# The opening of a cross-attention and FP4 feed-forward kernel: low parts of the down weights by a subtraction on VectorE, and a new order of the opening

## What is computed

```python
def xattn(q, k, v, Wt, Wp, Wg, Wz, gamma, beta):      # k = v = ctx
    t, p, g = Wt @ v, Wp @ q, Wg @ k                  # 256x256 weights over the channels
    att = sum(p * g over each of 8 groups) * 0.125    # one number per group
    y = Wz @ (att * t)                                # per group
    y = (y - mean) / sqrt(var + eps)                  # over a group's channels and columns
    return y * gamma + beta + v
def ffn(x, w_gate, w_up, w_down):                     # 512 -> 1408 -> 512
    q = fp4_quant_dequant                             # blocks of 16, scale max|x|/6, grid 0..6
    h = silu(q(x) @ q(w_gate).T) * (q(x) @ q(w_up).T)
    return q(h) @ q(w_down).T
x = x + xattn(layernorm(x), ctx, ctx, ...)
x = x + ffn(layernorm(x), ...)
```

## Time and profile before

| | us |
|---|---|
| median of 3 runs | 1725.51 (1724.89 to 1725.58) |
| profiled execution, its own time | 1728.17 |
| span of the profile | 1726.1 |
| TensorE busy in the span | 1681.8 |
| VectorE busy | 1503.2 |
| ScalarE busy | 828.3 |
| GpSimd busy | 671.4 |

### The profile page before, as it was taken

How to read it: one execution, slowest core, us unless ns; L and a number is a source line. 1 busy time by engine, 2 the same in 40 slices (tenths; PEclk the granted TensorE clock), 3 DMA queues, 4 the chain that set the end, 5 groups by cost and what they waited for, 6 DMA issues and landing times.

```text
span 1726.1 us, 27850 instructions
## 1 busy us (share of the span) xinstructions
PE 1681.8 (97%) x8723; PEld 920.6 (53%) x8723; DVE 1503.2 (87%) x2607; ACT 828.3 (48%) x1492; POOL 671.4 (39%) x877
## 2 busy tenths in 40 slices
PE   4799999999999999999999999999999999999999
PEld 3675455555555555555555555555555555555544
DVE  7978888888988888898888889888888988888887
ACT  5675445444445544444554444455444445544422
POOL 6764334333443433334343333434333343433310
PEclk9899999999999999999999999999999999999999
DMA  8033534344343434434343343434344343434321
GB/s 259 34 62 78 107 70 94 90 89 99 90 99 77 94 90 89 99 90 99 77 94 90 90 99 90 100 77 94 90 90 98 90 101 75 94 90 90 75 53 46
DMA packets 411863, 155.86 MB, mean 90 GB/s; under 512 B 383169, under 2 KB 383937, under 8 KB 411841
## 3 DMA queue, kind: packets, MB, share of 16 engines
q1 hardware_dynamic: 396064, 125.17, 34.2%
q10 hardware_dynamic: 15776, 30.41, 5.5%
HBM read 43.03 MB, written 16.78 MB: 35 GB/s over the span
## 4 chain that ended last, share of the span: by engine, by line
PE 94%; DMA 2%; DVE 2%; ACT 1%; issue 1%; POOL 1%; SPq 0%; DVEq 0%; ACTq 0%; POOLq 0%
PE pairs L588 51%; PE work L599 26%; PE work L530 5%; PE work L544 3%; PE ubank L563 3%; PE work L563 2%; PE pairs L645 1%; DMA hT_parts<-raw 1%; PE pairs L637 1%; DMA early<-in_L_xattn_Wg 1%; DMA qT<-q_parts 0%; PE pairs L530 0%; PE pairs L647 0%; POOL raw L1972 0%; PE pairs L618 0%
## 5 line engine op out<-in xcount | busy, mean ns | idle before, releaser
L588 PE MATMUL pairs<-w_gate_hi,xT_parts 128*128 128x512 f16 (+1 forms) x1536 | 555.4, 362 | 1.5 <-DMA xT_parts<-raw 1.5
L588 PE MATMUL pairs<-w_up_hi,xT_parts 128*128 128x512 f16 (+1 forms) x1536 | 554.7, 361 | 0.0
L599 PE MATMUL work<-w_parts,hT_parts 128*128 128x512 f16 x2079 | 458.9, 379 | 2.6 <-DMA hT_parts<-raw 2.6
L599 PEld LDWEIGHTS work<-w_parts,hT_parts 128*128 128x128 f16 x2079 | 203.3, 99 | 238.1 <-issue 2.6
L588 PE MATMUL pairs<-w_up_lo,xT_parts 128*128 128x512 f16 (+1 forms) x768 | 277.5, 361 | 0.0
L588 PE MATMUL pairs<-w_gate_lo,xT_parts 128*128 128x512 f16 (+1 forms) x768 | 277.4, 361 | 0.0
L588 PEld LDWEIGHTS pairs<-w_gate_hi,xT_parts 128*128 128x128 f16 x1536 | 152.7, 99 | 163.0 <-issue 14.4
L588 PEld LDWEIGHTS pairs<-w_up_hi,xT_parts 128*128 128x128 f16 x1536 | 150.4, 98 | 146.1
L1026 ACT ACTIVATE early<-pairs,w_unit 128x512 f32<-128x512 f32 (+1 forms) x192 | 124.9, 651 | 160.2 <-PE pairs L588 160.2
L924 ACT CAST raw<-hq 128x704 f16<-128x704 f32 x126 | 98.1, 779 | 161.0 <-DVE hq L1290 159.6
L1498 DVE SCALAR_TENSOR_TENSOR h<-pairs,w_unit,early 128x512 f32<-128x512 f32 (+1 forms) x192 | 135.1, 704 | 41.5 <-ACT early L1026 36.4
(11 more groups left out here) (190 smaller groups left out, 2817.8 us busy)
## 6 DMA issues: line engine op xcount, KB each, us to landing
out<-raw SPq DMA_DIRECT2D x64, 256.0 KB, 2.1
c_in<-in_ctx ACTq DMA_DIRECT2D x29, 512.0 KB, 4.5
x_in<-in_x ACTq DMA_DIRECT2D x29, 512.0 KB, 5.2
raw<-in_L_ffn_w_down SPq DMA_DIRECT2D x2, 1408.0 KB, 7.0
raw<-in_L_ffn_w_gate SPq DMA_DIRECT2D x2, 1024.0 KB, 6.7
w_parts<-in_L_ffn_w_up SPq DMA_DIRECT2D x2, 1024.0 KB, 10.9
c_in<-in_ctx SPq DMA_DIRECT2D x3, 512.0 KB, 4.4
x_in<-in_x SPq DMA_DIRECT2D x3, 512.0 KB, 7.3
```

The costliest lines, as they stand in the source:

```text
L588: mm = pe.matmul(pairs[:, pair, n, 0:b - a], xT[s][part][:, k, :], w1[n][wpart][:, k, a:b], start=(k == 0 and part == 0 and wpart == 0), s ...
L599: mm = pe.matmul(obank[:, :], hT[part][:, k, :], w2[wpart][:, k, :], start=(k == 0 and part == 0 and wpart == 0), stop=(k == KH - 1 and pa ...
```

## The change

Down sets (22 to 33) lose `turn_again` and `weights_lo`. In their place `down_lo(k)` on VectorE subtracts the hi part in SBUF from the bank in PSUM and writes the lo part; it waits for `weights_hi(k)`, and counts on a new semaphore `down_lo_done`. Gate and up sets stay as they are. The same banks are used, so `turn_weights(k)` of a down set now waits for `down_lo(k - 2)`, and the last group of `second_hidden` for all 12.

```diff
-                at_least(pe, w_lo_done, k - 1)
+                at_least(pe, w_lo_done, min(k - 1, DOWN_SET0))
+                at_least(pe, down_lo_done, k - 1 - DOWN_SET0)
...
-                    pe.wait_ge(w_lo_done, ALL_SETS)
+                    pe.wait_ge(down_lo_done, ALL_SETS - DOWN_SET0)
...
+            def down_lo(k):
+
+                _, cols, dst = weight_sets[k]
+                dve.wait_ge(w_hi_done, k + 1)
+                nc.vector.tensor_tensor(dst[1], pairs[:, 1, k % 2, 0:len(cols) * P].rearrange("p (c n) -> p c n", n=P), dst[0],
+                                        ALU.subtract).then_inc(down_lo_done, 1)
...
             def x1_moments(t):
+                if isinstance(t, int) and 0 < t < 4:
+                    dve.wait_ge(ln2_mean, t)
```

More of the change, by code:

```diff
@@ L734, in _ @@
             turn_weights(6)
+            turn_again(6)
             turn_weights(7)
-            turn_again(6)
+            turn_weights(8)
             turn_again(7)
-            turn_weights(8)
             turn_again(8)
             turn_weights(9)
+            turn_again(9)
             turn_weights(10)
-            turn_again(9)
             turn_weights(11)
@@ L746, in _ @@
             turn_weights(12)
+            turn_again(12)
             turn_weights(13)
-            turn_again(12)
             turn_again(13)
@@ L1652, in _ @@
             x_add(0)
+            x_back(0)
+            x_quant(0)
             weight_round(15)
-            x_back(0)
-            max_down(2)
-            max_down(3)
-            x_quant(0)
             scales_down(1)
@@ L1677, in _ @@
             weight_round(21)
+            ln1_moments(2, 1)
+            down_lo(22)
             weight_round(22)
-            x_y(1)
+            ln1_means(2)
+            down_lo(23)
             gated(0, 0, 2)
+            x_back(1)
             h_first(0)
-            x_add(1)
+            down_lo(24)
             h_scales(0, 0)
-            x_back(1)
             x_quant(1)
@@ L1687, in _ @@
             x_lo(1)
-            weight_round(23)
-            ln1_moments(2, 0)
+            down_lo(25)
             sum_pg(1, 0)
             sum_pg(1, 1)
+            h_snap_add(0)
             copy_group(1)
+            down_lo(26)
             h_units(0, 0)
+            h_snap_back(0)
             variance(1)
-            ln1_moments(2, 1)
-            ctx_power(2)
-            h_snap_add(0)
-            h_snap_back(0)
-            h_quant(0, 0)
-            residual(2, 0)
-            h_quant(0, 1)
-            ln1_means(2)
-            gated(1, 1, 0)
-            x1_moments(2)
+            h_quant(0, 0)
+            weight_round(23)
+            h_quant(0, 1)
+            down_lo(27)
+            down_lo(28)
+            gated(1, 1, 0)
+            down_lo(29)
+            down_lo(30)
+            residual(2, 0)
+            ctx_power(2)
+            x1_moments(2)
+            h_lo(0, 0)
+            normalise1(2, 0)
+            residual(3, 1)
+            h_lo(0, 1)
+            down_lo(31)
             x1_mean(2)
-            h_lo(0, 0)
-            h_lo(0, 1)
+            down_lo(32)
+            normalise1(2, 1)
+            down_lo(33)
+            x1_moments(3)
             normalise2(2)
             x_first(2)
-            residual(3, 1)
-            gated(1, 1, 1)
-            normalise1(2, 0)
-            normalise1(2, 1)
             x_scales(2)
             x_y(2)
+            gated(1, 1, 1)
             gated(1, 1, 2)
```

375 lines of the change are left out of this document (178 added, 197 removed).

## The result

Time after: 1738.83 us, median of 4 runs (1736.17 to 1739.6), against 1725.55 for the kernel before in the same comparison; ratio 1.0068, 95% interval 1.0056 to 1.0080. The change makes the kernel 0.7% slower. The forecast was 1717.9 us, faster.

What follows compares the result with a forecast made beforehand. TensorE's matmuls were taken to bound the part after 92 us, VectorE's chain right beneath. The 12.2 us saved, less waits of 2, 1.5 and 1.1, gave 7.6: 1725.51 - 7.6 = 1717.9 us, range 1709 to 1726.

Steps and rivals of the forecast that it cites:

- the new order up to `x_lo(0)`: Opening up to 90.08 us: x-first loads cost 0, between 3 lost and 3 won; 2 us of VectorE's idle time won.
- the premise on TensorE: After 92 us TensorE's matmuls are the bound, so dropping twelve `turn_again` saves 12.2 us if nothing else comes late.
- VectorE's addition: Twelve subtractions after 92 us add 7.7 us to VectorE, up to 14.0 if stretched by GpSimd; 7.7 taken.
- VectorE had 15.8 us idle: From 92 to 157 us VectorE's idle time; shortened by 12.2 it leaves 3.6, and 7.7 don't fit.
- fourth rival: Subtractions add in full to VectorE's chain, body begins 7.7 us later, TensorE waits at `output(0)` and `output(1)`: 1733.2, chance 0.08.
- waits for attention: Opening: `gram(0)` and `mixed(0)` ahead of the first weights remove these waits, part of the 2 us taken.
- Steps 1 to 6: From `first_hidden(0)` at 91.4 to `output(0)` at about 142 instead of 149.57, by the new lists: 7.6 us earlier.
- waits of "2, 1.5 and 1.1 us": New TensorE waits before `second_hidden(0)`, between sets 30 and 31, and before `second_hidden(2)`, taken off the 12.2 us.
- as nothing, since TensorE hides it: From 92 to 157 us ScalarE, busy 43.21 of 65 us, loses twelve copies; their effect was counted as nothing.
- The low clock: Rival: a second half-clock stretch at the waits of steps 3 to 5 costs 4.4 us: 1722.3, chance 0.04.
- The loops: Each iteration costs TensorE's own time, 200.00 of 200 us busy, which the change doesn't touch.

Runs made afterwards that it cites:

- e10: Kernel before without the twelve `turn_again` of the down sets; ScalarE copies the same bank again for the low parts, no subtraction on VectorE: 1725.99 us, ratio 0.9992.
- e1: Kernel before with the twelve subtractions alone, in its own lists, no other call moved: 1732.12 us, ratio 1.0022.
- e2: Kernel after with `turn_c(0)` moved on SP's queue ahead of the load of the first half of down: 1732.85 us, ratio 1.0034.
- e6: Kernel after with `turn_c(0)` ahead of down's load, and `gram(0)`, its copy and `sum_pg(0, s)` behind the first weights: 1732.5 us, ratio 1.0035.
- e5: Kernel after with SP's whole list of loads and transposes from kernel before, other four lists as changed: 1745.73 us, ratio 1.0109.
- e12: Kernel before with subtractions for sets 30 to 33 only, and `gated(1, 1, 0)` ahead of `residual(2, 0)` and `ln1_means(2)` on VectorE: 1730.05 us, ratio 1.0010.
- e11: Kernel before with the subtraction for the last four down sets (30 to 33) alone; 22 to 29 keep the second turn: 1730.15 us, ratio 1.0021.
- e9: Kernel before with the twelve subtractions, TensorE still doing 88 second-turn matmuls that nobody reads, without the 12 that subtract: 1733.47 us, ratio 1.0037.
- e7: All five lists of kernel before up to about set 18, from there the changed kernel's order with subtractions: 1731.23 us, ratio 1.0029.
- e3: Kernel after with down's low parts made by `turn_again` on TensorE and ScalarE's copy, at chosen places, no subtraction: 1758.28 us, ratio 1.018.
- e4: Kernel after with each `down_lo` replaced by a ScalarE copy of the bank, so low parts are copies of hi parts: 1738.71 us, ratio 1.0064.
- e8: Kernel before with the twelve subtractions, and `sum_pg(1, s)` and `copy_group(1)` moved earlier on VectorE: 1732.77 us, ratio 1.0038.

## Why the prediction was wrong

`output(0)` was forecast at 142 and came at 159.55 us. Of these 17.5 us, 11.3 were lost before the first hidden group (102.75 for 91.4) and 6.2 after it (56.8 for 50.6); 1.7 more went at the end. The first piece is the new order up to `x_lo(0)`, the second the premise on TensorE.

**"If nothing else came late, this would be the gain, 12.2 us", "TensorE's matmuls are the bound of the second part".** This step carried the whole gain, and it failed. The count was right (12 times less, 100 matmuls), the place on the path was not. TensorE's 64.31 of 65 us showed only that it was never without work, not that the work was wanted at that time. With ScalarE's copies kept, the 12.2 us were worth 1.4 (e10).

A part of this stood in the trace of before. The earlier trace rows begin at 117.60; the chain that ended last has no work of TensorE in the 25 us above that line. It runs through GpSimd and the transpose of q, for which `gram(1)` waits 0.50 us:

```profile
96.37 2.59 POOL raw L1980
...
106.24 2.59 POOL raw L1972
...
110.44 6.91 DMA qT<-q_parts
```

The second turns of sets 22 to 25, from 107.57 to 116.50, 4.2 of the 12.2 us, stand beside this chain. In e1, without them, `gram(1)` began at 117.62 all the same. For the other 8 us the chain is TensorE's own, and could not show what lay beneath: an engine that works through a gap has no wait there.

**VectorE's addition.** 7.7 us was right: the twelve took 545 to 690 ns, and e1's came to 7.6. None was stretched, though the one at 121.94 (0.67 us) ran wholly beneath a multiply of GpSimd (2.59 us from 121.57), while VectorE's operation with both inputs in SBUF at 112.98 took 3.02 us beneath the like. The Trainium skill, SBUF — State Buffer, section Who interferes with whom, says that an instruction of VectorE with at most one input in SBUF does not contend with GpSimd, and one with two does; the trace agrees. (The residual of the earlier trace rows ended 0.55 us after GpSimd's multiply, not with it.) What was wrong is the step that hid the addition: "VectorE had 15.8 us idle". That idle time was the same chain seen from VectorE. In the old order 5.2 us came on top (e10 to e1), so the fourth rival's mechanism ("the subtractions add to VectorE's chain in full", chance 0.08) was much nearer than the forecast.

**"The new order up to x_lo(0): I take 0, between 3 lost and 3 won", with 2 us of idle time on top.** Measured: `x_lo(0)` at 98.80 instead of 89.26, `first_hidden(0)` at 102.75 instead of 91.4. The 1 MB ahead of gate cost VectorE nothing by itself: its first maxima came 3.6 us later (9.95 instead of 6.36), but `weight_round(0)` at 26.08 instead of 25.92. The loss is the transpose of c. The diff said that it went behind q's and behind half of down, and the prediction priced neither, only the removal of "waits for attention"; and it took `gram(0)` ahead of `u_rows` as a gain, when this made TensorE, and three engines behind it, wait for that transpose. 5.9 us of the loss are shown to be this (e2). The rest, some 3 us at the first hidden group (98.14 in e2's profile, 95.03 before), stays open. `gram(0)`'s place shows nothing in the time (e6, where the mark is at 96.86), SP's list can't be tried alone (e5), and the granted clock alone moves this mark by as much (e12's 92.14).

**Steps 1 to 6, waits of "2, 1.5 and 1.1 us".** From `first_hidden(0)` to `output(0)` 50.6 us were forecast and 56.8 measured. Two of the waits named do appear, before set 31 and before `second_hidden(2)`, with 1.49 and 1.16 us as priced. Missing in the steps are those for ScalarE and GpSimd: 0.97 for `w_up_lo`, 1.94 for `rowst`, 0.88 for `att`. ScalarE had been counted "as nothing, since TensorE hides it"; with TensorE thinned out it was no longer hidden. All waits are 8.7 us instead of 4.6.

**The low clock, chance 0.04.** It came, at waits of 1 to 2 us that I had thought harmless: 0.58 and 0.74 over 135 to 145 us are 3.4 us at most, and `second_hidden(0)` alone took 2.2 us longer. After 92 us it came in the opening of every experiment but e11, where the clock stayed at 1.00 after a wait of 3.20 us. The Trainium skill, TensorE: Matmul & The Clock Gate, section HAM oscillation, says that waits between bursts of matmuls bring the lower clock back; the traces agree but for e11's, and the prediction was wrong to set it aside.

**The loops** were as before up to the last iteration. That the end would lose another 1.7 us was in no step.

## What to carry to other kernels

A full engine is not a bound: before you count its work as time, look for what else ends in the stretch, and try it. Read the chain that ended last over the whole stretch and not only where it suits. The cheapest proof is a run like e10, which leaves the work out; it would have shown 1.4 us where 12.2 were counted. Then read what ends the waits that come up, since what was put in for the work can be among it. In a hand-written order follow each moved DMA on its queue, and whoever is placed in front of its landing: one transpose behind one load was half of this change's loss.

## What the runs showed of the hardware

- A granted clock of 0.50, the lower of TensorE's two levels (1.2 GHz), needs no long pause: in e1 it held for the 10 us from 130 to 140 after waits of 2.29, 1.31, 0.90 and 3.37 us that ended between 117 and 131; in e9 a mean of 0.86 over 10 us followed one of 2.19. The filler matmuls of e9 didn't prevent it.
- The same calls with the same wait go either way. In kernel before TensorE waits 2.10 us before 49.67, and the granted clock is 0.54 in 50 to 60 us; in e12 it waits 2.10 us before 50.26, in e7 before 50.19, and it is 1.00 in both. The first hidden group starts some 3 us earlier for it (92.14 in e12, 95.03 before), so a mark in one profile each tells apart only what is larger than that.
- The spread of a kernel's runs goes with this clock. Ten runs of kernel before with a mean clock of 1.000 took 1724.4 to 1725.4 us, those at 0.996 took 1728.4 to 1729.6; e1's took 1728.8 to 1728.9 at 0.998 (three runs) and 1732.9 to 1734.4 at 0.993 (three runs). e10's lowest run is 2.6 us below the lowest of kernel before beside it, its median 0.1 above.
- The end of the program has such a place as well. Kernel before (1.47 us) and e3 (1.51) wait for the last x tile and keep the clock; the other twelve wait 2.4 to 2.5 us. In eight of them (after, e1, e2, e4, e7, e9, e11, e12) a granted clock of 0.83 over 10 us follows, in four (e5, e6, e8, e10) it stays at 1.00. One profile each doesn't tell what decides there.
